# Two more pixel pairs folded together on VectorE before the projection of a vision tokenizer

## What is computed

```
q = _ln(reduce_feats, ln_q_w, ln_q_b) @ Wq.T           # one query per patch
kv = _ln(unf, ln_kv_w, ln_kv_b) @ Wkv.T                # keys and values of its 16 pixels
attn = softmax(einsum('bhpd,bhpnd->bhpn', q * scale, k))
aggre = einsum('bhpn,bhpnd->bhpd', attn, v)            # sum of 16 weighted values
return reduce_feats + aggre @ proj_w.T + proj_b
```

## Time and profile before

| | |
|---|---|
| median of 3 runs | 881.12 us (879.34 to 882.15) |
| the profiled execution | 881.01 us, its span 879.2 us |
| PE busy | 838.2 us (95%) |
| DVE busy | 717.9 us (82%) |
| POOL busy | 524.4 us (60%; nearly all of it before 560 us) |
| ACT busy | 483.5 us (55%) |
| granted TensorE clock, mean | 0.990 of full speed |

### The profile page before, as it was taken

The page is one execution under the profiler, slowest core; times in us unless marked ns, Lnnn a source line. Parts: engine busy times, 40 slices in busy tenths (PEclk is TensorE's granted clock), DMA queues, the critical chain, the costliest instruction groups (busy, mean ns, idle before and its releaser), DMA issues.

```text
span 879.2 us, 23479 instructions
## 1 busy us (share of the span) xinstructions
PE 838.2 (95%) x9144; PEld 360.6 (41%) x9144; DVE 717.9 (82%) x1189; ACT 483.5 (55%) x782; POOL 524.4 (60%) x387
## 2 busy tenths in 40 slices
PE   5799999999999999999999997898999999999996
PEld 2134334344344343343343443464444444444442
DVE  5788888888888888888888888894788788788785
ACT  3646456455454464564554554358666566566562
POOL 2699999999999999999999964101121121121110
PEclk9999999999999999999999998999999999999999
DMA  9588998989989989999899764000000000000000
GB/s 374 158 240 252 260 283 245 263 267 260 275 250 260 286 242 259 278 250 263 256 253 264 217 168 111 2 2 2 0 13 13 25 13 13 25 13 13 25 13 36
DMA packets 70560, 141.60 MB, mean 161 GB/s; under 512 B 5440, under 2 KB 5440, under 8 KB 69440
## 3 DMA queue, kind: packets, MB, share of 16 engines
q1 hardware_dynamic: 70464, 140.21, 55.4%
HBM read 68.88 MB, written 4.19 MB: 83 GB/s over the span
## 4 chain that ended last, share of the span: by engine, by line
PE 39%; POOL 37%; issue 7%; DVE 7%; ACT 4%; DMA 3%; SPq 2%; POOLq 1%; DVEq 0%; ACTq 0%
POOL sb_rows L497 11%; POOL sb_prodv L604 7%; POOL sb_rows L502 6%; PE ring L1207 5%; POOL sb_wgt L592 4%; PE ring L1177 4%; POOL sb_rows L504 3%; POOL sb_score L586 3%; PE ring L952 3%; PE bank_ms L1219 3%; DMA sb_wbc<-sb_wgt 3%; SPq L545 2%; PE bank_ms L924 2%; PE qp L991 2%; PE qp L1162 2%
## 5 line engine op out<-in xcount | busy, mean ns | idle before, releaser
L952 PE MATMUL ring<-sb_arena,sb_wqkv 64*64 64x512 f32 x2048 | 254.1, 599 | 2.3 <-DVE sb_prodk L1349 1.5
L1380 DVE TENSOR_TENSOR sb_prodv<-ring,sb_wbc 128x1024 f32<-128x1024 f32 x128 | 151.8, 1206 | 43.6 <-DMA sb_wbc<-sb_wgt 25.4
L1349 DVE TENSOR_TENSOR sb_prodk<-ring,sb_qbuf 128x1024 f32<-128x1024 f32 x128 | 150.6, 1218 | 22.3 <-PE ring L952 16.8
L648 POOL TENSOR_TENSOR sb_parts_q<-sb_arena,sb_const 128x512 fp32r<-128x512 f32 x15 | 15.6, 1039 | 245.6 <-DVE sb_arena L1585 194.4
L497 POOL TENSOR_TENSOR sb_rows<-sb_arena 128x2048 f32<-128x2048 f32 x31 | 142.2, 4586 | 15.8 <-DVE sb_sum L489 15.8
L692 ACT ACTIVATE sb_xsq<-sb_arena 128x2048 f32<-128x2048 f32 x64 | 118.6, 1901 | 2.0 <-DMA sb_arena<-x 2.0
L952 PEld LDWEIGHTS ring<-sb_arena,sb_wqkv 64*64 64x64 f32 x2048 | 66.3, 132 | 115.6 <-issue 72.3
L991 PEld LDWEIGHTS qp<-sb_prodv,sb_tok_w 64*64 64x64 f32 x3072 | 93.1, 137 | 40.4 <-issue 40.2
L991 PE MATMUL qp<-sb_prodv,sb_tok_w 64*64 64x128 f32 x3072 | 98.8, 276 | 5.2 <-POOL sb_prodv L604 5.2
L604 POOL TENSOR_TENSOR sb_prodv<-sb_prodv 128x256 f32<-128x256 f32 x128 | 92.8, 735 | 10.7 <-DVE sb_prodv L1380 10.7
L663 ACT ACTIVATE sb_means<-sb_sum 128x256 f32<-128x256 f32 x32 | 13.3, 416 | 146.9 <-POOL sb_sum L507 143.1
(11 more groups left out here) (248 smaller groups left out, 1450.1 us busy)
## 6 DMA issues: line engine op xcount, KB each, us to landing
sb_arena<-x SPq DMA_DIRECT2D x64, 1024.0 KB, 7.4
sb_wbc<-sb_wgt SPq DMA_DIRECT2D x256, 256.0 KB, 5.7
out<-sb_arena SPq DMA_DIRECT2D x16, 256.0 KB, 2.0
sb_rest_w<-rest_w SPq DMA_DIRECT2D x1, 950.5 KB, 21.3
sb_const<-const SPq DMA_DIRECT2D x1, 264.5 KB, 3.0
sb_tok_w<-tok_w SPq DMA_DIRECT2D x1, 260.5 KB, 2.9
sb_const<-const SPq DMA_DIRECT2D x1, 256.0 KB, 21.6
```

The lines of the kernel that those rows point to most:

```text
L952: mm = pe.matmul(ring[slot][C * half:C * half + C, i, :], image_block(w, i), x[C * i:C * i + C, m, half, c], start=True, stop=True)
L1349: dve.tensor_tensor(by_pixel(prodk[:, c]), by_pixel(ring[c % 2][:, :, :]), q[:, :, None, :].to_broadcast([P, 2, N_PIX, G32]), ALU.mult).th ...
L1380: dve.tensor_tensor(prodv[:, :, :, G32 * c:G32 * (c + 1)], by_pixel(ring[k % 2][:, :, :]), by_pixel(wbc[:, c]), ALU.mult).then_inc(values_ ...
```

## The change

Pixels 6 and 7 of the weighted values are added onto pixels 4 and 5, by one DVE instruction per unit over all patches (512 elements per partition, two inputs in SBUF, one output in SBUF). It stands last in DVE's step, behind `query_scaled`. PE then projects ten pixels, those numbered 0 to 5 and 8 to 11 (`SUMMED`), six in the first part of the projection and four in the second. The first part also waits for the new addition, `pairs_added`.

```
-N_PRE = 4
+N_PRE, N_PAIR = 4, 2
 N_SUM = N_PIX - N_PRE
+SUMMED = tuple(range(0, N_SUM - N_PRE - N_PAIR)) + tuple(range(N_SUM - N_PRE, N_SUM))
...
                 if lo == 0:
                     pe.wait_ge(values_weighted, NC * u + NC)
+                    pe.wait_ge(pairs_added, u + 1)
...
-                if hi == N_SUM:
+                if hi == len(SUMMED):
                     pe.wait_ge(pixels_added, NC * u + NC)
-                for n in range(lo, hi):
+                for k in range(lo, hi):
                     for i in range(2):
                         for half in range(2):
                             rows_of = slice(C * half, C * half + C)
                             mm = pe.matmul(qp[C * i:C * i + C, half, 3 * PT:4 * PT], image_block(projw, half),
-                                           prodv[rows_of, i, n, :], start=(n == 0), stop=(n == N_SUM - 1))
+                                           prodv[rows_of, i, SUMMED[k], :], start=(k == 0), stop=(k == len(SUMMED) - 1))
...
-                    project(n - 1, 0, 8)
+                    project(n - 1, 0, 6)
...
-                    project(n - 1, 8, N_SUM)
+                    project(n - 1, 6, len(SUMMED))
...
+            def add_pairs(u):
+
+                dve.wait_ge(values_weighted, NC * u + NC)
+                onto = prodv[:, :, N_SUM - N_PRE - 2 * N_PAIR:N_SUM - N_PRE - N_PAIR, :]
+                dve.tensor_tensor(onto, onto, prodv[:, :, N_SUM - N_PRE - N_PAIR:N_SUM - N_PRE, :], ALU.add).then_inc(pairs_added, 1)
...
                 if nxt2:
                     query_scaled(n + 2)
+                add_pairs(n)
```

More of the change, by code:

```diff
@@ L248, in build @@
         pixels_added = sem("pixels_added")
+        pairs_added = sem("pairs_added")
         projected_mm = sem("projected_mm")
@@ L1057, in last_step @@
                 values(n, m, 0)
-                project(n - 1, 0, N_SUM)
+                project(n - 1, 0, len(SUMMED))
                 values(n, m, 1)
@@ L1063, in last_step @@
                 drive(0, 3)
-                project(n, 0, N_SUM)
+                project(n, 0, len(SUMMED))
             for n in range(UNITS - 1):
```

## The result

The changed kernel takes 889.73 us (median of 4 runs, 888.74 to 890.49) against 880.23 us for the kernel before (4 runs). The ratio is 1.0105, with a 95% interval of 1.0091 to 1.0119: 1% slower. The forecast was 892.0, in a range of 884 to 899. The profiled execution took 888.74 us, its span 887.0 us, 7.8 longer than before.

A forecast was written before the change was run, and what follows sets the result against it. The prediction took POOL to bound the loop. From 881.0 us, 13.05 lost on POOL, less 1.3 given back and 0.8 at the end, made 892.0 us, in a range of 884 to 899.

The forecast's parts named there:

- POOL bounds the loop: Loop: POOL's own work plus 0.28 us sets the period of 16.13 us; relieving another engine doesn't shorten it.
- POOL loses 0.45 us a unit to the addition: POOL's pixel additions before its patch sum: 0.45 us lost each step (bounds 0.19 and 0.71), 13.05 us in 29.
- The 0.28 added for the larger size: POOL's loss per step: 0.28 us, less a little, added to 0.19 for 512 instead of 256 elements.
- DVE's 0.7 us are hidden: End of DVE's `query_scaled`: the addition's 0.71 us fits 0.71 us of idle time there, 2.2 a period; cost nothing.
- given back: POOL's three long waits for DVE and a DMA in the loop shrink by up to 0.45 us each: -1.3 us.
- The end: Behind the loop's last patch sum, projections of units 30 and 31: -0.5 and -0.3, together -0.8 us.
- No loss on POOL: Rival: POOL stays the bound and loses nothing, only the end gains: 879.0 us; chance 0.08.
- PE is the bound: Rival: PE sets the loop's period, each of 31 projections gives 0.44 us: 867 us; chance 0.04.
- PE waits for the pairs: Rival: PE stalls 1.4 us before the projection's first part, period 17.1 us: 908 us; chance 0.05.
- Caught behind the patch sum: Rival: DVE's addition stands behind POOL's patch sum up to 4.59 us, period 3.1 longer: about 970 us; chance 0.03.

The follow-up runs named there:

- the relief alone: Kernel before with PE projecting ten pixels, without the addition and the wait for it (pixels 6 and 7 left out): 878.74 us, ratio 0.9976.
- the one-pair kernel: Changed kernel with only one pixel (7) added onto one (6), 256 elements on DVE, PE projecting eleven: 884.56 us, ratio 1.0046.
- the reduction of 1.23 us: Changed kernel with the two pairs folded by a DVE reduction with one SBUF input, sums written to their own place: 889.51 us, ratio 1.0099.
- the moved wait: Changed kernel with PE's wait for the pairs moved to the projection's second part (4 and 6 pixels): 890.69 us, ratio 1.0111.
- the late addition: Changed kernel with the addition moved behind the next step's second key products, PE waiting in the projection's second part (4 and 6 pixels): 1008.03 us, one run.
- the late place alone, by the reduction: Changed kernel with a one-SBUF-input reduction instead of the addition, behind the next step's second key products: 912.18 us, one run.

## Why the prediction was right

**POOL bounds the loop.** Right, and shown by the relief alone: period 16.06 with 14 us less work on PE. It was said too flatly that no relief of another engine shortens the period: PE was about 0.1 us from being the bound, and with the relief the loop was 2.1 us shorter in the one execution of each that was profiled.

**POOL loses 0.45 us a unit to the addition.** Right: 847 - 735 ns over four additions is 0.45, all of it on the third. The 0.28 added for the larger size, less a little, was right too: by the one-pair kernel (0.19) it is 0.26.

**DVE's 0.7 us are hidden.** Right for the changed kernel, but with less room than I wrote. I read 0.71 us of idle time at the spot and 2.2 in the period, and took the second for cover too. Only the first counts: the reduction of 1.23 us there cost 0.3 us a period. The addition with its wait took 1.06, and stayed hidden under a period of 16.5.

**The sum.** It gave +11 us. The profiled executions differ by 7.7, the medians by 9.5. In the loop, first to last patch sum, it is 477.45 - 468.08 = 9.4 instead of 13.05 - 1.3 = 11.75. Two terms were mis-sized. POOL's busy time grew by 11.61 us in 28 periods, 0.41 each and so 12.0 in 29, where 13.05 was said. And more is given back: POOL's idle time fell from 18.26 to 15.51 us, by 2.75 instead of 1.3. Its waits for DVE (1.4 us) and for a DMA (0.9) vanished whole, where I had counted at most 0.45 of each; the rest went from the short steps between its instructions. The end gained 0.7 (0.8 said): from the last patch sum to the end 374.8 us before and 374.15 after. The remaining 0.95 us is in front of the loop, where the first patch sum began at 35.35 instead of 36.30. I hadn't a term for it, and it doesn't look like the change's: the same start lies between 35.4 and 36.8 in the experiments, with the addition and without. So the sum is 3.3 us too high by the profiled executions and 1.5 by the medians (the profiled execution of the changed kernel is the fastest of its four), with the mechanism right.

**The rivals.** "No loss on POOL" is out by the rows, "PE is the bound" by the relief alone, "PE waits for the pairs" by the moved wait. "Caught behind the patch sum" didn't happen where the addition stands, but the late addition shows that the mechanism is real. Its period is 4.4 us over the kernel before, where 3.1 was said for being caught; the late place alone, by the reduction, makes 1.1 of it, so that 3.3 are left, with the lower clock in them.

## What to carry to other kernels

Before VectorE takes over a sum of two SBUF tensors, look at what GpSimd is doing at that moment. If GpSimd is the bound, each such instruction costs it time (here 0.19 us for 256 elements, 0.45 for 512), and if a long GpSimd instruction is running, VectorE stands until that is over (here 3.45 us instead of 0.68). Where the same sum can be had with one SBUF operand, as here by a reduction over a strided view, the loss goes away, if VectorE has the time at that very spot. And work taken from an engine that looks 100% busy buys next to nothing as long as another one's own work fills the period; the chain and the waits tell that, the busy share doesn't.

## What the runs showed beyond that

The bound before was double. POOL's period of 16.07 us and PE's, 15.98 by the estimate above, differ by less than the 0.22 us of one pixel in the projection, so that easing POOL by one pixel at PE's cost made the kernel 0.23% slower. The granted clock late in the program can differ between executions of nearly the same kernel (0.96 and 0.99 over the last 134 to 138 us), and moves the time by 4 us, as much as the addition of one pixel pair costs.
